# Shifting where tiles lie in SBUF: small tiles reordered and three gaps resized in a six-stage transformer kernel

## The reference

```python
x = x + 0.5 * L0_ffn(layernorm(x))    # hidden 1536, weights rounded to fp8, scales
x = x + L0_attn(layernorm(x))         # 16 query heads, 4 key/value heads, rope, biases
x = x + 0.5 * L0_ffn(layernorm(x))
x = x + 0.5 * L1_ffn(layernorm(x))    # hidden 2048, SiLU gate
x = x + L1_attn(layernorm(x))         # 16 heads, causal
x = x + 0.5 * L1_ffn(layernorm(x))
```

## The kernel before

| tile | start before | start modulo 512 |
|---|---|---|
| x | 384 | 384 |
| minus_half, p_scale (4 bytes each) | 33152, 33184 | |
| wmem, raw0, tmp0, ident | 33216, 49600, 53696, 57792 | 448 |
| first tile of each stage | 60864 | 448 |
| s1a0: bo, v, e32, ow0, y, yT0, ysb0 | 155072, 159168, 163264, 193984, 198080, 202176, 212416 | 448 |
| s2f0: ds, dso0, w20, hB0 | 145344, 147392, 151488, 157632 | 448 |
| s3f1: h00, h30, wd0, a00, graw00 | 151488, 177600, 185792, 193984, 210368 | 448 |
| s4a1: v, e32, ow0, y | 161216, 177600, 208320, 212416 | 448 |
| s5f1: graw00, h20, h00 | 93632, 110016, 142784 | 448 |
| s5f1: h40, g040, wd0, a00 | 161216, 185792, 198080, 206272 | 448 |

## Time and profile before

### The profile page before, as it was taken

The page is one execution under the profiler, slowest core; times in us unless marked ns, Lnnn a source line. Parts: engine busy times, 40 slices in busy tenths (PEclk is TensorE's granted clock), DMA queues, the critical chain, the costliest instruction groups (busy, mean ns, idle before and its releaser), DMA issues.

```text
span 2542.9 us, 45685 instructions
## 1 busy us (share of the span) xinstructions
PE 2445.9 (96%) x16544; PEld 1946.0 (77%) x16544; DVE 1748.7 (69%) x3608; ACT 1281.7 (50%) x2521; POOL 1505.6 (59%) x2045
## 2 busy tenths in 40 slices
PE   6999989999999999899999999999999989999999
PEld 4788767677767888688888888777777568888887
DVE  7787679888986444666565555788588966665555
ACT  6455346655664222555455443566466745454443
POOL 5333557767773334876677652666456876676663
PEclk9999989999999999999999999999999999999999
DMA  4212132131221110011111113333233211111112
GB/s 153 75 64 74 42 72 62 48 68 45 59 59 59 38 54 1 26 59 52 66 50 50 51 42 76 72 83 75 59 85 87 62 55 50 50 51 51 61 64 75
DMA packets 85841, 154.01 MB, mean 61 GB/s; under 512 B 17265, under 2 KB 26481, under 8 KB 85617
## 3 DMA queue, kind: packets, MB, share of 16 engines
q1 hardware_dynamic: 85616, 151.09, 20.9%
HBM read 87.58 MB, written 13.63 MB: 40 GB/s over the span
## 4 chain that ended last, share of the span: by engine, by line
PE 76%; DVE 8%; POOL 3%; issue 2%; ACT 2%; SPq 1%; DMA 1%; DVEq 0%; POOLq 0%; ACTq 0%
PE psum L1550 38%; PE psum L1601 23%; PE psum L1659 5%; PE psum L1696 4%; PE psum L1677 4%; DVE psum L2129 3%; PE psum L1707 2%; PE psum L1559 1%; POOL s4a1e L2323 1%; DVE x L2196 1%; SPq L2408 1%; POOL wmem L2286 0%; DVE s1a0rden L2168 0%; DVE s4a1rden L2168 0%; POOL s4a1e L2312 0%
## 5 line engine op out<-in xcount | busy, mean ns | idle before, releaser
L2129 DVE CUSTOM_DVE_ANT_0 psum<-psum,mask_q 128x512 f32<-128x512 f32 (+5 forms) x768 | 413.1, 575 | 92.1 <-PE psum L1659 89.9
L2082 DVE SCALAR_TENSOR_TENSOR x<-psum,x 128x512 f32<-128x512 f32 x256 | 176.8, 691 | 278.7 <-PE psum L1550 278.5
L1914 ACT ACTIVATE s4a1e<-psum,p_scale 128x384 f32<-128x384 f32 (+5 forms) x384 | 205.1, 579 | 84.3 <-PE psum L1677 80.8
L1914 ACT ACTIVATE s1a0e<-psum,p_scale 128x384 f32<-128x384 f32 (+5 forms) x384 | 200.9, 577 | 70.3 <-PE psum L1677 68.7
L1550 PE MATMUL psum<-s5f1wd,s5f1a 128*128 128x512 f32 x768 | 194.2, 389 | 3.0 <-DVE s5f1a L2074 2.2
L1550 PE MATMUL psum<-s3f1wd,s3f1a 128*128 128x512 f32 x768 | 195.4, 390 | 0.9 <-issue 0.9
L1601 PE MATMUL psum<-s3f1h,wmem 128*128 128x512 f32 x768 | 190.6, 391 | 3.5 <-DVE s3f1h L2043 2.3
L1601 PE MATMUL psum<-s5f1h,wmem 128*128 128x512 f32 x768 | 189.7, 390 | 0.0
L2323 POOL TENSOR_TENSOR s4a1e<-s4a1e 128x896 f32<-128x896 f32 (+3 forms) x128 | 164.6, 1286 | 17.6 <-ACT s4a1e L1914 6.2
L2323 POOL TENSOR_TENSOR s1a0e<-s1a0e 128x896 f32<-128x896 f32 (+3 forms) x128 | 164.6, 1286 | 17.1 <-ACT s1a0e L1914 5.8
L2294 POOL TENSOR_TENSOR x<-x,s0f0dso 128x512 f32<-128x512 f32 x64 | 89.9, 1426 | 136.6 <-DVE s0f0dso L2023 136.6
(11 more groups left out here) (233 smaller groups left out, 6200.4 us busy)
## 6 DMA issues: line engine op xcount, KB each, us to landing
raw<-in_down SPq DMA_DIRECT2D x76, 256.0 KB, 3.9
s1a0qst<-s1a0qs SPq DMA_DIRECT2D x96, 128.0 KB, 2.4
s4a1qst<-s4a1qs SPq DMA_DIRECT2D x96, 128.0 KB, 2.4
s4a1kst<-s4a1ks SPq DMA_DIRECT2D x96, 128.0 KB, 2.4
s3f1graw<-in_gate SPq DMA_DIRECT2D x32, 256.0 KB, 3.1
s3f1graw<-in_up SPq DMA_DIRECT2D x32, 256.0 KB, 3.1
s5f1graw<-in_gate SPq DMA_DIRECT2D x32, 256.0 KB, 3.0
s5f1graw<-in_up SPq DMA_DIRECT2D x32, 256.0 KB, 3.1
```

The costliest lines, as they stand in the source:

```text
L1914: act.activation(T[s]["e32"][:, begin_ + z * pw:begin_ + (z + 1) * pw - skip], src, ACT.Exp, bias=p_scale[:]).then_inc(sem["exp"], 1)
L2082: dve.scalar_tensor_tensor(x[:, tile, :], src, 0.5, x[:, tile, :], ALU.mult, ALU.add).then_inc(sem["x_add"], 1)
L2129: dve.tensor_tensor_reduce(scores, scores, mask_q[:, first:first + pw], -1.0, -MASKED, ALU.add, ALU.min, T[s]["negmax"][n % 2][:, column:c ...
```

## The change

The tiles keep their shapes and the program keeps its instructions, their order and their waits. What changes is the order in which small tiles are asked for, and the sizes of the gaps:

```diff
-LOW_GAP, V_GAP, SMALL_GAP, COLUMN_GAP = 1152, 384, 512, 96
+LOW_GAP, V_GAP, SMALL_GAP = 1056, 508, 536
...
         x = sbuf(ctx, "x", [P, NT, D])
-        minus_half = sbuf(ctx, "minus_half", [P, 1])
-        p_scale = sbuf(ctx, "p_scale", [P, 1])
         wmem = sbuf(ctx, "wmem", [P, 2, 4, D], F32R)
...
         rstd = sbuf(ctx, "rstd", [P, NT])
+        minus_half = sbuf(ctx, "minus_half", [P, 1])
+        p_scale = sbuf(ctx, "p_scale", [P, 1])
         minus_max = sbuf(ctx, "minus_max", [P, 1])
...
-                    def columns_of():
+                    def scales_of():
                         t["gs"] = sbuf(sc, f"{tag}gs", [P, HIDDEN[kind] // P])
                         t["us"] = sbuf(sc, f"{tag}us", [P, HIDDEN[kind] // P])
-
-                    def scales_of():
                         t["ds"] = sbuf(sc, f"{tag}ds", [P, D])
...
                         a_of()
                         scales_of()
-                        columns_of()
                     elif kind == "f0":
...
-                        columns_of()
-                        gap(COLUMN_GAP)
                         scales_of()
                         weights_of(2, 0)
...
                         t["rope"] = {n: sbuf(sc, f"{tag}rope{n}", [P, SEQ]) for n in "qk"}
+                        t["bcol"] = sbuf(sc, f"{tag}bcol", [P, 4 + 1 + 1])
                         t["bo"] = sbuf(sc, f"{tag}bo", [P, D])
+                    t["negmax"] = [sbuf(sc, f"{tag}negmax{i}", [P, ST + CT]) for i in range(2)]
                     t["mrow"] = [[sbuf(sc, f"{tag}mrow{i}{p}", [ST, P], F32R) for p in range(2)]
...
-                    t["negmax"] = [sbuf(sc, f"{tag}negmax{i}", [P, ST + CT]) for i in range(2)]
-                    if kind == "a0":
-                        t["bcol"] = sbuf(sc, f"{tag}bcol", [P, 4 + 1 + 1])
```

## The result

The changed kernel takes 2558.42 us (median of five, 2556.44 to 2560.45) against 2544.66 for the kernel before, run beside it (2539.68 to 2545.5): a ratio of 1.0061, with a 95% interval of 1.0051 to 1.0073. It is slower by 0.6%, where I had given 0.57 to no change and had ended the range at 2557.

What follows compares the result with a forecast made beforehand. TensorE's rate in each stage was taken to bound the kernel. Instructions, all start-address moves and DMA were each 0 us, summing to 0 against the profiled 2544.66 us; the median forecast was 2543.4 us, range 2537.5 to 2557.

Steps and rivals of the forecast that it cites:

- Instructions, waits: Whole kernel: the same 45685 instructions in the same order behind the same waits, nothing queued behind a new wait; 0 us.
- Kind 1: Tiles such as wmem and all moved in s0f0, s2f0, s3f1, s4a1, shifted by 64 or multiples of 128 bytes; 0 us.
- faster by kind 1: Rival: shifting wmem against h removes 13.3 ns a matmul, in all stages using wmem, ending at 2496 us; chance 0.04.
- Kind 2: Tiles in s1a0 and s5f1 moved to 32 above a multiple of 64; taken as 0, range 10.9 and 53.9 us.
- The price of 9.5 us in s5f1: Upper bound: 1344 matmuls there, with h and g or wd and a, each pay 7.1 ns for one more 64-byte piece.
- The narrow products, my 43 us: s1a0's products with values and ones, read in 128-byte runs, three pieces instead of two: at worst 43 us more; chance 0.05.
- DMA: Loads landing and ysb, mrow, wmem read at other starts: taken as 0, with 1.4 us if a tenth were passed on.
- the meeting of engines: Rival: GpSimd or ScalarE shifts change who comes first in attention stages, 2.8 us either way or 5.6; chance 0.11.

Runs made afterwards that it cites:

- h_plus128: The kernel before with LOW_GAP 1184 and V_GAP 352, so only h0, h1 and h2 of s3f1 move, by +128 bytes; 2547.46 us, ratio 1.0011.
- small_gap: The kernel before with SMALL_GAP 536 instead of 512, moving only h4-h6, g4-g6, wd and a of s5f1 together by +96 bytes; 2549.44 us, ratio 1.0019.
- rest_only: The changed kernel with minus_half and p_scale put back ahead of wmem, so wmem, raw, tmp and ident stay at 448 modulo 512; 2561.72 us, ratio 1.0056.

## Why the prediction was wrong

**Instructions, waits and what bounds the kernel: right.** There are 45685 instructions again, and TensorE's two largest waits went from 26.0 and 6.8 us to 25.5 and 6.6. That the only question was whether an address changes how fast TensorE streams was right too.

**Kind 1 is the step that failed: "On the path: 0."** I put its bounds at nothing more above, and a gain below. The rows I read showed VectorE and GpSimd indifferent to x's start, and I noted that TensorE never reads x. I had no row for TensorE, and so a bound upward was missing, though I had one downward for just this case, wmem shifted against h. The reason I gave, that 226.7 ns stands alike for slices at any 512-byte step and while six kinds of tiles alternate, was empty: 512 is a multiple of the period of 256, and all six kinds started at the same byte modulo 512. The constancy of that number proved only that the start had never been varied. What the runs showed in place of 0: moves of kind 1 alone make s2f0 3.7 us and s3f1 7.1 us longer, 10.8 us together, and h_plus128, with one such move of three tiles, costs 3.9 us in s3f1.

**The sign of the "faster by kind 1" rival.** It looked at the right thing, the start of wmem against that of h, and had the direction wrong: the layout before is the best of those tried at 512 columns. For the 256-column products the rival was right in direction, with 2.2 ns a matmul (102.2 less 100.5 us over 768 in s4a1), not 13.3.

**Kind 2.** The price of 9.5 us in s5f1 came to 5.8, and not for its reason. Tiles at 32 modulo 64 cost nothing by themselves: in the last part of a round of s5f1, where wd with a and h with g take turns and all lie at 32, six matmuls take 1.36 us in the changed kernel as well, from 2257.59 us on, and h with g rose only 0.6 us over the stage. What s5f1 pays is the switching between tiles that moved and tiles that did not: small_gap gives +4.7 us for that alone, with rounds of 30.31 us. The shift of wmem on top adds nothing that can be seen: rest_only, without it, has +5.4 us and rounds of 30.31, the changed kernel +5.8 and 30.30. That 5.8 us came out inside the 9.5 I had allowed for another reason is luck. The narrow products, my 43 us, pay nothing: 5.18 us a block at every difference.

```profile
2256.22 1.37 PE psum L1595 x6
2257.59 1.36 PE psum L1544 x6
2258.95 1.36 PE psum L1595 x6
2260.32 1.36 PE psum L1544 x6
```

**DMA and the meeting of engines.** No run shows either above the few us by which the attention stages scatter.

The 215.7 ns for 512 columns of the Trainium skill (page "TensorE: Matmul & The Clock Gate", section "Wait — 56ns, not 53.3ns?") agree with bfloat16 here, 215.8. With float32r the best that any start gave is 226.7, so the 11 ns that I priced in that rival come with the data type, and no start tried gives them back.

## What to carry to other kernels

Where TensorE is the bound and its matmuls are float32r, 512 columns wide with 128 stationary columns, put stationary and moving tiles, and all moving tiles that alternate within a run of matmuls, at the same start modulo 256 bytes, and check it by the distance between matmuls (here 226.7 ns for 512 columns, and 228.8 to 234.3 where it was not so). A tile order or a gap that "only" shifts tiles is a change of the kernel's speed, and a row that never varies is evidence of nothing about the setting that was never varied. For narrower matmuls measure again: at 256 columns 64 bytes apart was better than 0.

## What the hardware did that I had not expected

- Distance between float32r matmuls of 512 columns: 226.7 ns with starts equal modulo 256, 228.8 with the stationary 64 bytes below, 232.4 to 234.3 at the other multiples of 32.
- It has a memory: after a switch of the moving tile's start (modulo 256), equal pairs run some 4 ns slow on average for up to ten matmuls, in much the same sequence each time, and after groups of 256 columns for one to eight; after unequal pairs of the same shape on the same moving tile they are back after four at most.
- bfloat16 (215.8 ns) and narrow float32 matmuls show nothing of it, and the free difference moves from 0 to 96 bytes when the stationary operand has 64 columns in place of 128.
